# First pair of banks of a direct band read out by ScalarE, ahead of the next seed

## The reference, cut to what matters

```python
def reference(x, ...):
    v = _gn(x)                                   # 32 groups of 2 channels
    res = conv3x3(v, W_id, b_id)                 # every image
    cA, cH, cV, cD = _swt2_level3(v[0])          # image 0 only
    ...                                          # two attentions, concatenated: dmt
    out = leaky_relu(conv3x3(dmt, W_enc, b_enc), 0.01)
    return x + out + res
```

## Time and profile before

| what | us |
|---|---|
| median of 3 executions | 1816.95 (1816.91 to 1819.03) |
| the profiled execution, its own time | 1814.87 |
| its span, first to last instruction | 1813.1 |
| TensorE matmuls busy | 1761.4 (97%) |
| VectorE busy | 1450.2 (80%) |
| ScalarE busy | 1238.6 (68%) |
| stage `main` | about 812 to 1808 |

### The profile page before, as it was taken

One profiled execution on the slowest core, in us unless ns is written; L12 is line 12 of the kernel. 1 busy time (PEld: TensorE's weight loads), 2 busy tenths in 40 slices (PEclk: granted clock), 3 DMA queues, 4 the chain that ended last, 5 costly groups with the idle time before them and its releaser, 6 DMA issues. The chain is left out here.

```text
span 1813.1 us, 69228 instructions
## 1 busy us (share of the span) xinstructions
PE 1761.4 (97%) x31540; PEld 1470.2 (81%) x31540; DVE 1450.2 (80%) x1926; ACT 1238.6 (68%) x1339; POOL 545.5 (30%) x365
## 2 busy tenths in 40 slices
PE   9999999999999999989999999999999999999997
PEld 9997999999999999965577797767966756967676
DVE  5665578778777887668989889888889888888886
ACT  5555666666666666667776777767776767766774
POOL 0005788888888888640000000000000000000000
PEclk9999999999999999999999999999999999999999
DMA  8884399888888888458998998998989989989994
GB/s 186 245 296 126 122 274 227 212 219 216 212 215 215 215 215 206 100 125 204 235 234 223 239 239 226 240 240 229 238 224 236 247 213 232 242 219 230 249 234 140
DMA packets 132964, 391.84 MB, mean 216 GB/s; under 512 B 49884, under 2 KB 50656, under 8 KB 118464
## 3 DMA queue, kind: packets, MB, share of 16 engines
q1 hardware_dynamic: 132672, 387.43, 82.7%
HBM read 258.88 MB, written 128.45 MB: 214 GB/s over the span
## 5 line engine op out<-in xcount | busy, mean ns | idle before, releaser
L1766 PE MATMUL ps<-big,tail 64*64 64x448 f16 x3840 | 323.3, 353 | 11.8 <-DVE ps L1961 7.8
L1766 PE MATMUL ps<-pool_of 64*64 64x448 f16 x5184 | 302.5, 352 | 7.9 <-DVE pool_of L1625 4.2
L1766 PE MATMUL ps<-pool_of,tail 64*64 64x448 f16 x4896 | 300.1, 349 | 0.7 <-issue 0.7
L1766 PE MATMUL ps<-big,pool_of 64*64 64x448 f16 x3552 | 278.5, 352 | 17.1 <-DVE ps L1961 11.9
L1292 DVE BATCH_NORM_STATS2 pool_of<-big 128x6 f32<-128x448 f32 x392 | 232.2, 616 | 76.4 <-DMA big<-in_x 76.3
L1766 PEld LDWEIGHTS ps<-pool_of 64*64 64x64 f16 x5184 | 196.2, 107 | 68.0 <-issue 10.1
L1766 PEld LDWEIGHTS ps<-pool_of,tail 64*64 64x64 f16 x4896 | 189.6, 106 | 59.3 <-issue 1.3
L1066 PE MATMUL ps<-pool_of 112*128 112x246 f16 x1344 | 218.8, 271 | 1.7 <-DVE pool_of L1280 0.8
L1070 PE MATMUL ps<-pool_of 112*128 112x168 f16 x1344 | 217.8, 243 | 0.0
L1766 PEld LDWEIGHTS ps<-big,tail 64*64 64x64 f16 x3840 | 169.0, 107 | 57.9 <-DVE ps L1961 10.4
L1069 PE MATMUL ps<-pool_of 112*128 112x90 f16 x1344 | 201.3, 206 | 0.0
(11 more groups left out here) (252 smaller groups left out, 3809.8 us busy)
## 6 DMA issues: line engine op xcount, KB each, us to landing
out<-tail SPq DMA_DIRECT2D x448, 224.0 KB, 3.6
big<-in_x SPq DMA_DIRECT2D x392, 224.0 KB, 5.2
pool_of<-in_x SPq DMA_DIRECT2D x139, 560.0 KB, 7.4
tail<-in_x SPq DMA_DIRECT2D x69, 560.0 KB, 7.4
pool_of<-row_filtered SPq DMA_DIRECT2D x110, 224.0 KB, 4.0
row_filtered<-big SPq DMA_DIRECT2D x2, 6272.0 KB, 22.8
pool_of<-in_x SPq DMA_DIRECT2D x30, 392.0 KB, 7.1
row_filtered<-big SPq DMA_DIRECT2D x4, 1568.0 KB, 9.2
```

Of the source, the lines that this page charges most:

```text
L1766: mm = pe.matmul(psum[bank + r][C * k:C * k + C, 0:NT], wt[i % 2][lanes, h, s, kx, :], v[u][lanes, rows_of(k), kx:kx + W], start=False, st ...
```

## The change

The read of group 0 moves from VectorE to ScalarE; the read of group 1 stays on VectorE.

- ScalarE gets `read_first(j)`: one activation (identity with a scale per lane) in place of VectorE's multiplication, with the same operands and the same two waits. It stands after `full` and ahead of `seed_direct(q+2, 0)`.
- VectorE's `read_direct(j, g)` becomes `read_second(j)`, for group 1 only and in the same place at the end of the step.
- The semaphore `g_read` becomes a pair, one per group, since two engines now raise it. `seed_direct(·, g)` waits for its own group's, the store for both.
- `neighbour_sums` gets a wait on `sums_split`, which VectorE's own `sums_low` raises in the step before.

```diff
-        g_read = sem(top, "g_read")
+        g_read = [sem(top, f"g_read{g}") for g in range(2)]
...
             if j:
-                act.wait_ge(g_read, 2 * j - 1 + g)
+                act.wait_ge(g_read[g], j)
...
             def store_direct(j):
-                sp.wait_ge(g_read, 2 * j + 2)
+                for g in range(2):
+                    sp.wait_ge(g_read[g], j + 1)
                 store(*direct(j), 0)
...
+            def read_first(j):
+                i, b = direct(j)
+                if j:
+                    act.wait_ge(stored[0], 64 * j)
+                act.wait_ge(g_done, 2 * j + 1)
+                act.activation(stage[0][:, :, 0, :], g_bank[0], ACT.Identity, scale=lane(m_out, i)).then_inc(g_read[0], 1)
...
                 if q >= 0 and q + 2 < ND:
                     full(act, q + 2)
+                if q + 1 < ND:
+                    read_first(q + 1)
                 if q + 2 < ND:
                     seed_direct(act, q + 2, 0)
...
                 k = place_w(j)
+                if j:
+                    dve.wait_ge(sums_split, j)
                 landed(dve, k)
...
-            def read_direct(j, g):
+            def read_second(j):
                 i, b = direct(j)
                 if j:
                     dve.wait_ge(stored[0], 64 * j)
-                dve.wait_ge(g_done, 2 * j + g + 1)
-                dve.tensor_scalar(stage[0][:, :, g, :], g_bank[g], lane(m_out, i), None, ALU.mult).then_inc(g_read, 1)
+                dve.wait_ge(g_done, 2 * j + 2)
+                dve.tensor_scalar(stage[0][:, :, 1, :], g_bank[1], lane(m_out, i), None, ALU.mult).then_inc(g_read[1], 1)
...
-                if q + 1 < ND:
-                    read_direct(q + 1, 0)
                 if q >= 0 and q + 2 < ND:
                     split(dve, q + 2)
...
                 if q + 1 < ND:
-                    read_direct(q + 1, 1)
+                    read_second(q + 1)
```

## The result

The changed kernel took 1802.39 us in the median of 4 executions (1799.27 to 1805.93), the kernel before 1817.72 (4 executions). The ratio is 0.9916, 95% interval 0.9895 to 0.9936. The forecast was 1798.2 within 1791.0 to 1805.0, and faster. The profiled execution took 1799.27 us, 15.6 less than the profiled one of before, with a span of 1797.5.

What follows compares the result with a forecast made beforehand. TensorE, busy 97%, was taken as the bound, so only its waits for VectorE's seed_odd in building pairs could be won: 13.9 us of waits plus 4.8 of clock, 18.7 off 1816.95, giving 1798.2 us, range 1791.0 to 1805.0.

Steps and rivals of the forecast that it cites:

- VectorE's queue between build and split: Last stage's building steps: the first-pair read there, 1.07 us of queue, delays seed_odd, for which TensorE waits.
- 2.14 us a pair, the first step's microsecond carried into the second: Six pairs of building steps: seed_odd ends 1.07 us sooner in the first step, 2.14 in the second; 12.8 us together.
- The pair at 1206: Building pair with only one wait for seed_odd: one read counts, 1.07 us gained, bounds 1.07 and 2.14.
- ScalarE at no cost: 56 reads of 1.01 us on ScalarE, covered by its slack before even_rows: cost 0, otherwise 1.04 us a step.
- The added and moved waits at nothing: Waits on earlier stores, sums_split, g_read and the store's second read: each 0, the first read at most 0.3 either way.
- The clock, 4.8 us: Pairs 2, 6 and 7: three low-clock stretches behind longer waits vanish, 3 x 1.6 us; ends 0 and 4.8.
- the clock keeps falling: Rival: shorter waits still bring three low-clock stretches, so only 13.9 us is gained, 1803.1 us; chance 0.13.
- Sum: Whole kernel: 13.9 us of waits plus 4.8 of clock, 18.7 us off the median 1816.95, giving 1798.2.
- the half gain: Rival: ScalarE's order holds the second step's start, each pair gains one read, 7.5 us in all, 1809.5; chance 0.10.
- the DMA queues: Rival: DMA queues become the bound and later loads take back the gain, 1816 or so, no change; chance 0.06.
- the late store: Rival: ScalarE's new read waits for the previous band's late stores, 26 us slower, 1843; chance 0.05.
- The full gain: Rival: the 1.2 us left in six pairs vanish as well, 25.9 us gained, 1791.1; chance 0.06.

Runs made afterwards that it cites:

- e1: Against the kernel before: first-pair read moved to ScalarE only in the 14 building steps, VectorE keeping it in the other 42; 1798.31 us, ratio 0.989.
- e2: Against the kernel before: first-pair read moved to ScalarE only in the 42 steps without a build, VectorE keeping it in the 14 building steps; 1818.1 us, ratio 0.9997.
- e3: Against the kernel before: read moved to ScalarE only in the first step of each building pair; 1810.1 us, ratio 0.9941.
- e6: Changed kernel with the second half of an image's weights built at its sixth direct band instead of its fourth; 1799.33 us, ratio 0.989.
- e4: Changed kernel without the first read at all, half of each direct band's output left out; 1799.6 us, ratio 0.9897.
- e10: Repeat of the kernel before, for one more trace; one execution of 1817.87 us.
- e5: Repeat of the changed kernel; 1799.58 us, with the kernel before at 1818.56 beside it.
- e12: Another repeat of the changed kernel, for a third trace; 1800.91 us, with the kernel before at 1819.48 beside it.
- e8: Changed kernel with stores of a quarter of the bytes, each DMA writing one row of four; 1796.02 us, ratio 0.987.
- e9: Changed kernel with VectorE reading the first pair of banks again in four steps, those of two building pairs; 1806.22 us, ratio 0.992.
- e7: Kernel before with the second half of an image's weights built three steps later; 1814.72 us, ratio 0.9974.

## Why the prediction was right, point by point

- **VectorE's queue between build and split** as the limit: shown by e1 and e2. 14 reads make the gain, 42 make nothing.
- **2.14 us a pair, the first step's microsecond carried into the second**: pairs 1, 3 and 5 went from 37.55 to 35.42 in the mean, 2.13; e3 shows the carrying over by the 1.06 us between the two `diffs_low`. The left-over of 1.2 us came as forecast, 35.4 - 34.2, and e6 shows that some 0.7 of it was carried over from the first step by the queue.
- **The pair at 1206**: 37.78 became 36.67, 1.11 against 1.07. The wait of 1.01 us for the seed in its second step is gone whole; most of what keeps this pair over 34.2 are issue waits in its first step, 0.41 and 1.15 us, which the working did not look at.
- **ScalarE at no cost**: e4 shows none. The read's 0.99 us was 1.01 in the working, and the cover, 2.2 us left before `even_rows`, was 2.38.
- **The added and moved waits at nothing**: no row of the trace after has VectorE waiting for its own `sums_split`, and what grew is its wait for `full` in ordinary steps. No read on ScalarE waited for a store; one waited 0.8 us for TensorE.
- **The clock, 4.8 us**: the direction is right, and the size was partly luck. No low-clock stretch is left in the pairs of the changed kernel's traces, and the mean granted clock went from 0.9946 (34 executions) to 0.9976 (12); 0.0030 of 1800 us is 5.4, but that mean covers the whole span. By the traces the stretches in the last stage's steps 1 to 53 were 3, 2 and 3 (before, e10, e2) and became 1, 0 and 0 (after, e5, e12), which is 7/3 x 1.6 = 3.7 us a run; the forecast counted the three of one trace. The one left stands behind an issue wait of 2.20 us (in the step at 1603.58), as one in e1 stands behind an issue wait of 2.02. So it wasn't only the seed's waits that could bring it. For the rival "the clock keeps falling" the Trainium skill, "TensorE: Matmul & The Clock Gate", section on the clock gate, was quoted: the count of slow matmuls differs between runs of one kernel. The page says it of a kernel's start; the traces agree within the stage, with 3 stretches in the first trace of before and 2 in the second.
- **Sum**: 18.7 forecast; 15.3, 19.0 and 18.6 in the three comparisons of medians, 17.2 over all executions. Of the 2.9 us between 1798.2 and the mean of 1801.1, 1.3 lie in the median from which the forecast starts, 1816.95 against a mean of 1818.2. The traces say where the rest lies. Before, e10 and e2 have 267.8 us in the seven pairs and 678.6 in the 39 other steps in the mean; after, e5 and e12 have 248.9 and 680.6. The pairs gave 18.9, as the sum had it; the other steps, which it put at nothing, lost 2.0. That term is missing from the sum: issue waits, 11.8 us in the mean of the three against 9.5, and the low clock that followed one. The single traces differ by as much (677.6 to 683.5 us in the changed kernel), and so the loss itself is likely and not shown.
- **Rivals**: the half gain fell with e3, in which it had to be made on purpose; the DMA queues with the trace after itself, in which the ordinary steps stay at 17.1 us, and with e8; the late store with the trace. (In the working of that last one the fourth store, 2.3 us after 1371.18 and 3.7 to land, lands at 1377.2 and not at 1377.8; nothing hangs on it.) The full gain isn't what the change does, but what e6 adds to it, and even there the time follows only in part.

## What to carry to other kernels

If an engine is the limit only in a few steps, find those steps and what stands in its queue ahead of the late result there; whether moving that work helps elsewhere doesn't matter, and what it costs on the other engine is read from that engine's slack in the ordinary steps. Two heavy steps in a row add up where the second starts from the first one's last instruction: a microsecond saved in the first counts in both, and setting them apart takes away part of the rest. When waits of a nearly full TensorE are taken away, look at its other waits too: some that no releaser explains end a fixed time after a packet of the instruction queue, and a part of the gain may come back there. Repeat traces before a sum of such waits is compared, and take a term that hangs on chance, like stretches at the low clock, from more than one trace.

## What the runs showed of the hardware

- The granted clock fell to 0.50 for 3.4 us behind waits of TensorE of about 2 us, but not behind each: before, e10 and e2 together have 18 such waits for the seed and 8 stretches; e3 has one stretch, e9 none behind its two. Of nine issue waits of 1.9 to 2.3 us in all traces two had one (after, e1). At the stage's start e1, e2 and e6 have one each behind a wait of 2.7 to 3.1 us for ScalarE, e7 and e9 none behind 2.9 and 2.6. Behind waits for the seed of 1.2 us or less no stretch began in any trace.
- TensorE's waits "on issue" in the last stage, 0.2 to 2.3 us each, end 2.35 to 3.06 us after the start of a 16 KB packet on the instruction queue, all 184 over 0.25 us in 14 traces. They recur at fixed matmuls of the program (step 11 at 67, 17 at 74, 28 at 66, 45 at 64), with a size that changes from run to run, and add 9 to 16 us to a run. Stores of a quarter of the bytes (e8) left 8.9 us of them. Their sum scatters by 4.5 us between the changed kernel's own three traces, and its first four executions by 6.7 us.
- A read of two PSUM banks, 128 x 896 fp32 to SBUF with a scale, took 1.145 us on VectorE and 0.99 on ScalarE.
